# A two-layer graph network on one core: setup, middle and last stage rearranged, and the gathers' wait moved from a matmul to the transposes

## The chip, the cores and the metric

The kernel runs on one core of a Trainium2 chip. The time is that of the device in microseconds (us), the median of several runs. One further execution was taken with the hardware profiler, and all rows here are from that one. The engines are TensorE (PE, its weight loads PEld), VectorE (DVE), ScalarE (ACT), GpSimd (POOL) and SyncE (SP, which here only issues DMAs).

## The reference, cut to what matters

12,500 nodes with 16 features, and 412,500 edges sorted by their destination `dst`.

```python
h = relu(layernorm(x))
# layer 0: a weight matrix of each edge, from its 16 attributes
w = (relu(edge_attr_16 @ W1 + b1) @ W2 + b2).reshape(-1, 16, 16)
aggr = segment_sum(einsum('ei,eio->eo', h[src], w), dst)
out = aggr + h @ root + bias
x = x + relu((out - out.mean(0)) / sqrt(out.var(0) + 1e-5) * gamma + beta)
h = relu(layernorm(x))
# layer 1: messages from dst's features, summed by src
m = silu(einsum('ei,ej,ijh->eh', h[dst], edge_attr_8, W_msg_tp) * c1) @ W_msg_lin * c2
agg = segment_sum(m, src)
u = silu(einsum('ni,nh,ihk->nk', h, agg, W_upd_tp) * c3) @ W_upd_lin * c2
return x + h + u
```

## The kernel before

`build` (line 135) runs five stages with a barrier of all engines between them. Edges are worked on in G = 404 groups of 1,024, eight tiles of 128. Each engine's program is written out by hand in the order in which it runs, and engines wait for each other's semaphores (`wait_ge`, or `need`, which leaves out a wait for zero).

**Setup** (line 217). ScalarE issues the loads of `dst` and `src` in four chunks. VectorE makes the first layernorm (class `Norm`, line 543), whose square root ScalarE takes after it has rearranged W2 (line 438). `NodeLinear` (line 575) then multiplies all nodes in 13 chunks of 8 x 128 by b2 and `root`. Only then does VectorE turn `dst` into floats and find each group's least and greatest node (`front`, lines 342 to 348) and copy the turned `dst` out of PSUM (`dst_out`, line 350). GpSimd writes both index tables as int16 (`permute`), SyncE stores them, and the rows that layer 0 gathers (lines 278 to 281). `spread_in`, `spread_out` and a short chain give windows and the number of passes.

**Layer 0** (line 644). For each group GpSimd issues eight indirect DMAs, `xg <- gather_rows` (line 703), up to four groups ahead in a ring. TensorE's program for a group g (`body`, from line 834) is: `hidden` (line 801, W1, into ps_h), `edge_weights` (line 813, W2, into ps_w, four units of two tiles, a semaphore `wmm` after each unit), `hidden`, `edge_weights`, then `turn(g + 2)` (eight transposes of the attributes of a later group into ps_e, line 791, semaphore `e_turned`), and `scatter(g - 1)` (line 824, into ps_a). ScalarE evacuates ps_h with a relu (`relu`, line 742) and ps_e (`edges_T`, line 736). VectorE multiplies ps_w by the gathered rows and sums (lines 877 and 884). Two lines order the gathers:

```python
need(pool, q["msg_ready"], g - RING + 1)
need(pool, q["wmm"], 4 * (g - 2) + 3)
```

The second makes the gathers of group g wait for the third of the four units of group g - 2.

**Middle** (`between`, line 961). VectorE makes the batch norm, x + relu, and the second layernorm over [128, 104 x 16]. Then each node's 128 products Q = h @ Wmsg are made, and each is cut in three bf16 parts (high, middle, low), in 26 pieces of four node blocks: ScalarE writes high (line 1065), VectorE the residue (line 1039), ScalarE middle (line 1069), VectorE low (line 1044), SyncE stores Q (line 997).

**Layer 1** (line 1083). A block of its own copies and fills tables (`first_windows`, lines 1156 to 1168). In the loop SyncE loads four tiles for each group (`load`); after the loads of groups 1 and 2 it stores h and x by node (`by_node`, lines 1199 and 1201), and after group 3 reads them back in runs of nodes (`in_runs`). TensorE gathers Q rows by a one-hot product (line 1442), and sums messages by source in two ways (lines 1455 and 1468); GpSimd adds the first to tables in memory (line 1503).

**Last stage** (`finish`, line 1515). The tables are loaded and added (line 1588, half on VectorE, half on GpSimd), W_upd is loaded block-diagonally and rearranged by ScalarE (line 1682), and for 50 pairs of nodes per partition VectorE multiplies a PSUM bank by agg (line 1707) and reduces it (line 1714).

Of the kernel before, what the change touches and what calls it, by code (L numbers as in the profile page):

```python
# [26 lines left out]
P = 128  # L27
D = 16
# [41 lines left out]
def each_ring(engine, count, body, ring=4):  # L70


    for c in range(ring):
        body(c, c, 0)
    assert count % ring == 0
    with engine.Fori(0, (count - 2 * ring) // ring) as i:
        for u in range(ring):
            body(i * ring + (ring + u), u, i + 1)
    for u in range(ring):
        c = count - ring + u  # L80
        body(c, u, c // ring)
# [32 lines left out]
class Shapes:  # L114
    def __init__(self, n, e):
# [10 lines left out]
        self.BP = T * self.NC  # L126

# [10 lines left out]
def build(nc, x, src, dst, ea16, ea8, W1, b1, W2, b2, root, bias, gamma, beta,  # L138
          Wmsg, Wmsg_lin, Wupd, Wupd_lin, out):
    S = Shapes(x.shape[0], src.shape[0])  # L140
    with ExitStack() as ctx:
# [15 lines left out]
        k.q_rows = nc.dram_tensor("q_rows", (P * S.BP, 3 * P), bf16, kind="Internal").ap()  # L157
# [41 lines left out]
        with semaphores(nc) as sem:  # L199
            setup(nc, S, k, sem, src, dst, x, W1, b1, W2, b2, root, bias, gamma, beta)  # L200
        n_passes0 = nc.values_load(k.passes[0:1, 0:1], min_val=1, max_val=S.B // W + 1)
# [4 lines left out]
        with semaphores(nc) as sem, ExitStack() as c:  # L206
            k.Q = sb("Q", [P, S.BP, 3, P], bf16, c)
            between(nc, S, k, sem, c, Wmsg, Wmsg_lin, Wupd_lin)
        k.hp = sb("h_runs", [S.FP, S.FC, D], f32)
        k.xp = sb("x_runs", [S.FP, S.FC, D], f32)  # L210
        with semaphores(nc) as sem, ExitStack() as c:
            layer1(nc, S, k, sem, c, ea8, n_passes1)
        with semaphores(nc) as sem, ExitStack() as c:
            finish(nc, S, k, sem, c, Wupd, out)


def setup(nc, S, k, sem, src, dst, x, W1, b1, W2, b2, root, bias, gamma, beta):
# [3 lines left out]
    CH = len(chunks)  # L221
    with ExitStack() as c:
# [19 lines left out]
        pidx_i = sb("pidx_i", [P, 1], i32)  # L242
        rows = sb("rows", [P, S.BP, 2 * D], f32)
# [7 lines left out]
        reduced, masked = sem("reduced"), sem("masked")  # L251
# [5 lines left out]
        h_ready, rows_ready, stored = sem("h0_ready"), sem("rows_ready"), sem("rows_stored")  # L257
# [14 lines left out]
        def _(sp):  # L272
# [5 lines left out]
            sp.wait_ge(rows_ready, 1)  # L278
            sp.dma_start(k.rows[0:P * (S.B - 1), :].rearrange("(c p) f -> p c f", p=P),
                         rows[:, 0:S.B - 1, :]).then_inc(stored, 16)  # L280
# [8 lines left out]
            sp.wait_ge(stored, 32)  # L289
# [3 lines left out]
        def _(pool):  # L293
# [22 lines left out]
            for i, (g0, n) in enumerate(chunks):  # L316
                pool.wait_ge(s_flt, i + 1)
                permute(1, i, s_perm)
                if i == CH - 1:

                    pool.wait_ge(reduced, CH)
# [5 lines left out]
                else:  # L327
                    pool.wait_ge(d_flt, i + 1)
                permute(0, i, d_perm)

        @block.vector
        def _(v):
# [9 lines left out]
            def front(i):  # L342
                n = chunks[i][1]
                v.wait_ge(tab_in[0][i], landed(i))
                v.tensor_copy(flt[0][i][:, :], raw[0][i][:, :]).then_inc(d_flt, 1)
                v.wait_ge(d_flt, i + 1)
                v.tensor_reduce(lohi[0:n, i, 0:1], flt[0][i][:, :], X, ALU.min)
                v.tensor_reduce(lohi[0:n, i, 1:2], flt[0][i][:, :], X, ALU.max).then_inc(reduced, 1)

            def dst_out(i):  # L350
                g0, n = chunks[i]
                v.wait_ge(tr_d, i + 1)
                for h in range(2):
                    last = v.tensor_copy(k.dst[:, g0:g0 + n, 4 * h:4 * h + 4],
                                         ps_d[h][:, :, 0:n].rearrange("p t g -> p g t"))
                last.then_inc(ev_d, 1)
# [21 lines left out]
            v.wait_ge(nodes.packed, nodes.ALL)  # L378
# [9 lines left out]
            v.wait_ge(lin.taken, S.NC)  # L388
            v.sem_inc(rows_ready, 1)

            front(0)
            for i in range(1, CH):
                front(i)
                dst_out(i - 1)
# [11 lines left out]
            dst_out(CH - 1)  # L406
# [16 lines left out]
        def _(a):  # L423
# [10 lines left out]
            for i in range(CH):  # L434
                a.wait_ge(tab_in[1][i], landed(i))
                a.activation(flt[1][i][:, :], raw[1][i][:, :], ACT.Copy).then_inc(s_flt, 1)
# [3 lines left out]
            norm.scalar(a)  # L440
            lin.scalar(a)
            for i, (g0, n) in enumerate(chunks):
                a.wait_ge(tr_s, i + 1)
                for h in range(2):
                    last = a.activation(k.src[:, g0:g0 + n, 4 * h:4 * h + 4],
                                        ps_s[h][:, :, 0:n].rearrange("p t g -> p g t"), ACT.Copy)
                last.then_inc(ev_s, 1)

        @block.tensor
        def _(pe):  # L450
            pe.wait_ge(cst, 6)
            pe.wait_ge(nodes.packed, nodes.ALL)
            pe.wait_ge(h_ready, 1)
            lin.tensor(pe, k.ident[:, :])
            for i, (g0, n) in enumerate(chunks):
# [11 lines left out]
                last.then_inc(tr_d, 1)  # L467
            pe.wait_ge(ev_s, CH)
# [7 lines left out]
class NodesIn:  # L476


    def __init__(self, nc, S, k, sem, c):
        def sb(name, shape, dt):  # L480
# [4 lines left out]
        self.cleared, self.w_in, self.x_in, self.packed, self.dve, self.split = (  # L485
            sem(n) for n in ("cleared", "w_in", "x_in", "packed", "sn_dve", "w1split"))
        self.ALL = 16 * (2 * T + 6 + 6)
# [12 lines left out]
    def load_weights(self, sp, b1, W2, b2, root, bias, gamma, beta):  # L500
        k, packed = self.k, self.packed
# [1254 lines left out]
```

## Time and profile before

| | |
|---|---|
| median of 3 runs | 8827.98 us (8803.6 to 8840.02) |
| the profiled execution | 8860.82 us, span 8859.1 us |
| busy in it: PE, PEld | 7393.8 us (83%), 6326.6 us (71%) |
| DVE, POOL, ACT | 6501.9 us (73%), 5659.4 us (64%), 4441.1 us (50%) |
| mean granted clock of TensorE | 0.904 |

The span runs from the first to the last instruction. An engine's busy time is the union of its instructions; waits, branches and the issue of DMAs by SP and ACT are not in it. GpSimd's indirect DMAs are, for the time that it takes to make them. Shares over the whole span mix stages with different limits, so the stages are to be looked at one by one.

### The profile page before, as it was taken

How to read it: one execution, taken by the hardware profiler on the slowest of the kernel's cores; microseconds unless marked ns; L12 is line 12 of the kernel's file. 1: busy time of each engine (PE TensorE's matmuls, PEld its weight loads, DVE VectorE, ACT ScalarE, POOL GpSimd, SP SyncE). 2: the span in 40 equal slices, each digit the busy share in tenths (PEclk: the TensorE clock that was granted, in tenths of full speed). 3: DMA queues.
4: the chain of work that ended last, by engine and by line, in shares of the span. 5: the costliest groups of instructions: out<-in, count | busy, mean ns of one | idle time of the engine just before them, and what ended most of it. 6: DMA issues, size and time to landing. Idle time of an engine off the chain costs nothing. (4 is left out here: it accounts for less than half of the span.)

```text
span 8859.1 us, 189093 instructions
## 1 busy us (share of the span) xinstructions
PE 7393.8 (83%) x52097; PEld 6326.6 (71%) x52097; DVE 6501.9 (73%) x16875; ACT 4441.1 (50%) x8258; POOL 5659.4 (64%) x4883
## 2 busy tenths in 40 slices
PE   5777777777777777777777778599999999999997
PEld 4555665656665566665555656499999999999996
DVE  5555665656665566665565656799999999999997
ACT  2333333333333333333333333478888877778874
POOL 4555555555555555555555556288888888878884
PEclk8888888888888888888888888799999999999999
DMA  2000000000000000000000001444444455554443
GB/s 45 14 14 14 15 15 15 15 14 15 15 15 14 14 15 15 15 15 14 14 14 14 15 14 29 94 73 75 74 74 75 73 73 73 73 72 73 75 73 55
DMA packets 702285, 335.45 MB, mean 38 GB/s; under 512 B 422862, under 2 KB 645928, under 8 KB 702256
## 3 DMA queue, kind: packets, MB, share of 16 engines
q0 software_dynamic: 336128, 66.50, 12.4%
q1 hardware_dynamic: 364946, 265.19, 11.9%
q10 hardware_dynamic: 1182, 3.44, 0.1%
q8 instruction: 10, 0.16, 0.0%
q14 instruction: 19, 0.16, 0.0%
HBM read 301.49 MB, written 33.15 MB: 38 GB/s over the span
## 5 line engine op out<-in xcount | busy, mean ns | idle before, releaser
L703 POOL DMA_INDIRECT xg<-gather_rows,idx x3232 | 3082.3, 954 | 2385.2 <-PE ps_w L813 1140.4
L813 PE MATMUL ps_w<-W2s,hT 128*128 128x256 f32 x12928 | 3432.4, 417 | 446.2 <-issue 418.2
L813 PEld LDWEIGHTS ps_w<-W2s,hT 128*128 128x128 f32 x12928 | 2707.9, 210 | 1131.7 <-issue 687.0
L1503 POOL DMA_INDIRECT sums<-total,row x1616 | 2545.4, 1575 | 564.9 <-issue 440.8
L1468 PE MATMUL ps_wide<-hot_col,placed 128*128 128x392 f32 x12928 | 2439.0, 346 | 15.8 <-issue 9.6
L742 ACT ACTIVATE hT<-ps_h,b1c 128x512 f32<-128x512 f32 x1616 | 1018.6, 681 | 2721.4 <-remote 2163.2
L1468 PEld LDWEIGHTS ps_wide<-hot_col,placed 128*128 128x128 f32 x12928 | 2317.7, 196 | 29.8 <-issue 22.9
L877 DVE TENSOR_TENSOR prod<-ps_w,xg 128x512 f32<-128x512 f32 x1616 | 1095.9, 690 | 1118.0 <-remote 560.8
L1401 ACT ACTIVATE square<-iota_col,minus_col 128x784 bf16<-128x784 int16 x1212 | 1060.5, 937 | 88.5 <-issue 66.1
L1306 DVE SCALAR_TENSOR_TENSOR placed<-ps_r,src_r,halves 128x512 fp32r<-128x512 f32 x1616 | 1096.9, 740 | 0.1
L884 DVE TENSOR_REDUCE msg<-prod 128x32 f32<-128x512 f32 x1616 | 1059.1, 676 | 0.0
L801 PE MATMUL ps_h<-eT,W1p 96*128 96x512 bf16 x1616 | 562.9, 416 | 448.9 <-ACT eT L736 272.1
L1407 ACT ACTIVATE hot_col<-square,ones 128x2352 fp32r<-128x2352 bf16 x404 | 910.4, 2253 | 0.0
L908 DVE TENSOR_SCALAR hot<-iota,rel_t 128x256 bf16<-128x256 bf16 x3232 | 729.1, 298 | 113.2 <-DVE ea_res L860 58.7
L860 DVE TENSOR_TENSOR ea_res<-ea,ea_parts 128x128 f32<-128x128 f32 x404 | 116.7, 289 | 767.6 <-ACT ea_parts L723 542.2
L1442 PE MATMUL ps_q<-q_win,hotT 128*128 128x128 bf16 x9696 | 609.6, 220 | 28.0 <-DVE hotT L1245 28.0
L1263 DVE TENSOR_TENSOR prod<-ps_q,e 128x512 f32<-128x512 f32 x808 | 550.7, 682 | 80.6 <-issue 76.1
L801 PEld LDWEIGHTS ps_h<-eT,W1p 96*128 96x128 bf16 x1616 | 151.6, 99 | 626.9 <-issue 514.2
L1442 PEld LDWEIGHTS ps_q<-q_win,hotT 128*128 128x128 bf16 x9696 | 547.9, 98 | 29.1 <-issue 28.1
L1272 DVE TENSOR_REDUCE pre<-prod 128x64 f32<-128x512 f32 x808 | 546.8, 677 | 0.1
L824 PE MATMUL ps_a<-parts,hot 128*128 128x48 bf16 x6464 | 289.4, 184 | 300.7 <-issue 293.0
L824 PEld LDWEIGHTS ps_a<-parts,hot 128*128 128x128 bf16 x6464 | 230.1, 96 | 306.0 <-issue 298.8
(187 smaller groups left out, 4954.4 us busy)
## 6 DMA issues: line engine op xcount, KB each, us to landing
dst_row<-dst_rows SPq DMA_DIRECT2D x404, 256.0 KB
xg<-gather_rows,idx POOLq DMA_INDIRECT x3232
src_row<-src_rows SPq DMA_DIRECT2D x404, 128.0 KB
q_win<-q_rows SPq DMA_DIRECT2D x404, 96.0 KB
ea<-in_edge_attr SPq DMA_DIRECT2D x404, 64.0 KB
sums<-total,row POOLq DMA_INDIRECT x1616
e<-in_edge_attr SPq DMA_DIRECT2D x404, 32.0 KB
q_rows<-Q SPq DMA_DIRECT2D x13, 768.0 KB, 3.5
```

Of the source, the lines that this page charges most:

```text
L703: pool.indirect_dma_start(xg[r][:, t, :], None, k.rows, bass.IndirectOffsetOnAxis(ap=idx[r][:, t:t + 1], axis=0)).then_inc(xg_in[r][t], 16)
L742: a.activation(hT[s][:, j, :], ps_h[j][:, :], ACT.Relu, bias=k.b1[:, j:j + 1]).then_inc(q["relued"], 1)
L813: last = pe.matmul(bank[:, w, :, :].rearrange("p i o -> p (i o)"), hT[half][:, j, col:col + P], k.W2[:, j, :], start=(j == 0), stop=(j == 1))
L877: v.tensor_tensor(prod[u % 2][:, :, :, :], ps_w[u][:, :, :, :], xg[r][:, 2 * u:2 * u + 2, 0:D].unsqueeze(2).broadcast_to([P, 2, D, D]), AL ...
L884: v.tensor_reduce(msg[s][:, 2 * u:2 * u + 2, :], prod[u % 2][:, :, :, :], X, ALU.add).then_inc(q["reduced0"], 1)
L908: last = v.tensor_scalar(hot[s][:, t, :], k.iota[:, :], k.rel[:, bass.ds(g, 1), t:t + 1].rearrange("p g t -> p (g t)"), None, ALU.is_equal)
L1306: last = v.scalar_tensor_tensor(placed[s][:, w, :, :, :].rearrange("p r f a -> p r (f a)"), ps_r[:, :, :], src_r[:, bass.ds(g, 1), w], hal ...
L1401: last = a.activation(square[:, n, :], iota_col[:, :], ACT.Square, bias=minus_col[:, bass.ds(g, 1), WIDE - ACT_TILES + n])
L1407: a.activation(hot_col[s][:, WIDE - ACT_TILES:, :, :].rearrange("p w a b -> p (w a b)"), square[:, :, :].rearrange("p w b -> p (w b)"), AC ...
L1442: last = pe.matmul(ps_q[u][:, w, :, :].rearrange("p h j -> p (h j)"), hotT[s][:, t * P:(t + 1) * P], q_win[s][:, part * P:(part + 1) * P], ...
L1468: last = pe.matmul(ps_wide[:, 2 * r + a, 0:S.LC], placed[s][:, w, r * HR:(r + 1) * HR, :, part].rearrange("p r f -> p (r f)"), hot_col[s][ ...
L1503: pool.indirect_dma_start(k.sums[t], bass.IndirectOffsetOnAxis(ap=row[r][:, t:t + 1], axis=0), total[r][:, t, :], None, compute_op=ALU.add ...
```

## The change

- **Layer 0:** the gathers of group g wait for `e_turned` of g, the transposes at the end of TensorE's program for g - 2. The tables of sources that layer 1 opens with are made by VectorE in layer 0's last four groups.
- **Setup:** the least and greatest are found from the integers before the layernorm; ScalarE converts both tables and empties both sets of banks; TensorE turns them before `NodeLinear`; the relu is folded in the scaling; W2 is rearranged last; GpSimd copies h into the rows; these are stored in two halves.
- **Middle:** 98 node blocks and not 104; squares by ScalarE in halves; mask only on the last block; relu and the addition to x as one; Q in 25 pieces, every third high part by VectorE, all middle parts by ScalarE, all low parts by GpSimd; x is stored by node here; x + h is left to the last stage.
- **Layer 1:** no table block; the first `dst_row` load goes ahead of the wait for the windows; h is stored and read after the last group's loads; W_upd is loaded and rearranged by ScalarE before its first group; ScalarE's first two laps of four are written out.
- **Last stage:** tables in three pieces, loads issued by SyncE and ScalarE; from the fourth chunk on GpSimd folds each product to half its width before VectorE reduces it; four product buffers instead of two, reduce two behind.

```diff
@@ setup, VectorE @@
-            front(0)
-            for i in range(1, CH):
-                front(i)
-                dst_out(i - 1)
...
+            for i in range(CH):
+                least_greatest(i)
             v.wait_ge(nodes.x_in, 32)
             norm.vector(v, link, k.x, k.h)
             v.sem_inc(h_ready, 1)
-            v.tensor_copy(rows[:, :, 0:D], k.h[:, :, :])
@@ setup, ScalarE @@
+            for i in range(CH + 1):
+                if i < CH:
+                    to_float(1, i, s_flt)
+                    to_float(0, i, d_flt)
+                if i >= 1:
+                    out_of_psum(i - 1, k.src, ps_s, tr_s, ev_s)
+                    out_of_psum(i - 1, k.dst, ps_d, tr_d, ev_d)
+            norm.scalar(a)
+            lin.scalar(a)
@@ layer 0, GpSimd, gather(g) @@
                     need(pool, q["msg_ready"], g - RING + 1)
-                    need(pool, q["wmm"], 4 * (g - 2) + 3)
+                    pool.wait_ge(q["e_turned"], g + 1)
@@ layer 0, VectorE, end of body(g) @@
+                    if isinstance(g, int) and g >= G - RING:
+                        source_tables(g - (G - RING))
@@ middle, GpSimd @@
+        for piece in range(NP4):
+            b0 = 4 * piece
+            pool.wait_ge(n["q_mid"], piece + 1)
+            pool.tensor_tensor(k.Q[:, b0:b0 + 4, 2, :], res[piece % 3][:, :, :], k.Q[:, b0:b0 + 4, 1, :],
+                               ALU.subtract).then_inc(n["q_lo"], 1)
@@ middle, VectorE @@
+            if piece % 3 == 2:
+                v.wait_ge(lin.done, piece + 1)
+                v.tensor_copy(k.Q[:, b0:b0 + 4, 0, :], y).then_inc(n["q_hi_v"], 1)
@@ layer 1, SyncE @@
-                    if isinstance(g, int) and g == 1:
-                        by_node(k.h_rows, k.h)
-                    if isinstance(g, int) and g == 2:
-                        by_node(k.x_rows, k.x)
...
                 each(sp, G, body, head=4, tail=2)
+                store_by_node(sp, S, k.h_rows, k.h, q["h_stored"])
+                sp.wait_ge(q["h_stored"], 32)
+                in_runs(k.hp, k.h_rows)
@@ layer 1, ScalarE, before its first group @@
+                a.wait_ge(q["bdu_clear"], 1)
+                for b in range(T):
+                    a.dma_start(bd_hk[D * b:D * (b + 1), b, :],
+                                Wupd.rearrange("i h k -> i (h k)")).then_inc(q["bdu_in"], 16)
+                a.wait_ge(q["bdu_in"], 16 * T)
@@ last stage @@
-    SPLIT = ((0, MID), (MID, FC))
+    SPLIT = ((0, 2 * T), (2 * T, 6 * T), (6 * T, FC))
+    RU = 4
+    WHOLE = 3
...
+        for n in range(FOLD0, len(pairs)):
+            pool.wait_ge(upd_taken, n + 1)
+            need(pool, reduced, n - RU + 1)
+            y = prod[n % RU]
+            pool.tensor_tensor(fold[n % RU][:, :, :, :], y[:, :, :, 0:D // 2], y[:, :, :, D // 2:],
+                               ALU.add).then_inc(folded, 1)
```

On GpSimd, at the gathers of layer 0, the order stood thus before (`wmm` counts units of edge weights, `msg_ready` the messages done):

```order
L703 DMA xg<-gather_rows,idx 128x32 [waits idx_ready,wmm]
L703 DMA xg<-gather_rows,idx 128x32 x7
L76 UNCONDITIONAL_BRANCH
L76 ISA
L54 REGISTER_ALU [waits idx_ready]
L54 ISA [waits msg_ready]
L703 DMA xg<-gather_rows,idx 128x32 [waits wmm]
```

and now:

```order
L716 DMA xg<-gather_rows,idx 128x32 [waits idx_ready,e_turned]
L716 DMA xg<-gather_rows,idx 128x32 x7
L76 UNCONDITIONAL_BRANCH
L76 ISA
L54 REGISTER_ALU [waits idx_ready]
L716 DMA xg<-gather_rows,idx 128x32 [waits msg_ready,e_turned]
```

Nothing else in the loop moved: the same eight DMAs, another semaphore ahead of the first.

On ScalarE, at the first pieces of Q in the middle (`msg_xT` the turned nodes, `msg_po` the products in PSUM, `q_res` the residue), before:

```order
L620 ACTIVATE msg_xT<-msg_pt 128x128 [waits msg_turned] x2
L1065 ACTIVATE Q<-msg_po 128x4x128 [waits msg_done] x2
L1069 ACTIVATE Q<-q_res 128x4x128 [waits msg_taken] x2
L620 ACTIVATE msg_xT<-msg_pt 128x128 [waits msg_done,msg_turned]
L1065 ACTIVATE Q<-msg_po 128x4x128 [waits msg_done] x2
```

and now:

```order
L632 ACTIVATE msg_xT<-msg_pt 128x128 [waits msg_turned] x2
L1155 ACTIVATE Q<-msg_po 128x4x128 [waits msg_done] x2
L1145 ACTIVATE Q<-q_res 128x4x128 [waits msg_taken]
L632 ACTIVATE msg_xT<-msg_pt 128x128 [waits msg_done,msg_turned]
L1145 ACTIVATE Q<-q_res 128x4x128 [waits msg_taken]
L1155 ACTIVATE Q<-msg_po 128x4x128 [waits msg_done]
```

The middle part of a piece (L1145) now follows the high part of the next piece, and every third high part is gone from this engine.

On SyncE, after the second group's loads of layer 1, before (`h_rows` is h stored by node):

```order
L1191 DMA dst_row<-dst_rows 128x1024
L1194 DMA src_row<-src_rows 128x512
L1199 DMA h_rows<-hn 128x97x16
L1201 DMA h_rows<-hn 84x16
L1185 TENSOR_LOAD win_i [waits same_ready,gathered,hotT_ready,mult1]
```

and now:

```order
L1261 DMA e_1<-in_edge_attr 128x64
L1243 DMA dst_row<-dst_rows 128x1024
L1266 DMA src_row<-src_rows 128x512
L1258 TENSOR_LOAD win_i [waits same_ready,gathered,hotT_ready,mult1]
L1258 ISA x2
```

The two stores stand no more between the loads of groups 1 and 2 (nor those of x between 2 and 3).

## Rows read from the trace of the kernel before

**Rows 1.** By stage: length, busy us of each engine (instructions), TensorE clock, DMA share, GB/s.

```profile
84.00:5557.00 5473.00, 4212.03 (x24240) 3286.35 (x24240) 3345.43 (x9297) 1924.10 (x4040) 3082.34 (x3232) 0.86 0.09 15
5558.70:5594.00 35.30, 1.22 (x4) 1.00 (x4) 32.60 (x23) 2.48 (x3) 1.21 (x3) 0.50 0.02 2
5594.00:5641.30 47.30, 29.46 (x65) 11.49 (x65) 35.39 (x53) 31.06 (x65) 0.00 (x0) 0.90 0.64 216
5641.30:5651.40 10.10, 0.00 (x0) 0.00 (x0) 8.50 (x10) 0.00 (x0) 0.79 (x1) 0.50 0.00 1
...
5693.50:8752.10 3058.60, 3038.97 (x27320) 2958.61 (x27320) 2938.39 (x7227) 2431.40 (x4018) 2541.01 (x1615) 1.00 0.50 73
...
8763.70:8859.00 95.30, 63.11 (x191) 31.48 (x191) 70.00 (x117) 19.26 (x66) 9.58 (x5) 0.86 0.18 52
```

**Rows 2.** The page's group of layer 0's gathers: busy, mean ns, idle ahead of them.

```profile
L703 POOL DMA_INDIRECT xg<-gather_rows,idx x3232 | 3082.3, 954 | 2385.2 <-PE ps_w L813 1140.4
```

**Rows 3.** What ended the idle time ahead of those gathers: us in total, times.

```profile
  PE ps_w L813: 1140.4, 199
...
  remote: 335.4, 155
```

**Rows 4.** Timeline of GpSimd, start, us, idle before: first (once last) gather of groups.

```profile
1881.99 0.94 POOL L703 DMA_INDIRECT xg<-gather_rows,idx  x1 [2.41 <-remote]
...
1894.15 0.94 POOL L703 DMA_INDIRECT xg<-gather_rows,idx  x1 [2.41 <-remote]
...
1904.84 0.94 POOL L703 DMA_INDIRECT xg<-gather_rows,idx  x1 [0.47 <-issue]
...
1913.59 0.94 POOL L703 DMA_INDIRECT xg<-gather_rows,idx  x1 [0.30 <-issue]
1922.83 0.94 POOL L703 DMA_INDIRECT xg<-gather_rows,idx  x1 [8.29 <-PE ps_w L813]
```

**Rows 5.** Timeline of TensorE in the same stretch.

```profile
1901.64 0.61 PE L791 MATMUL ps_e<-identb,ea_parts 128*96 128x128 bf16 x8
...
1911.22 0.58 PE L813 MATMUL ps_w<-W2s,hT 128*128 128x256 f32 x1 [0.62 <-issue]
...
1916.15 3.73 PE L813 MATMUL ps_w<-W2s,hT 128*128 128x256 f32 x8 [0.81 <-issue]
```

**Rows 6.** Timeline of ScalarE in the same stretch.

```profile
1894.28 1.27 ACT L742 ACTIVATE hT<-ps_h,b1c 128x512 f32<-128x512 f32 x2 [5.30 <-PE ps_h L801]
...
1917.10 1.26 ACT L742 ACTIVATE hT<-ps_h,b1c 128x512 f32<-128x512 f32 x2 [16.55 <-remote]
```

**Rows 7.** Timeline of VectorE in the setup.

```profile
35.63 0.80 DVE L565 RECIPROCAL ln_sd<-ln_sd 128x104 f32<-128x104 f32 x1 [8.06 <-ACT ln_sd L571]
...
52.64 0.69 DVE L345 CAST fltd<-rawd 128x1024 f32<-128x1024 int32 x1 [0.15 <-DVE aggn L384]
...
70.77 0.15 DVE L397 CAST lohi_i<-lohi 128x8 int32<-128x8 f32 x1
```

**Rows 8.** Timeline of ScalarE and VectorE at Q's last pieces.

```profile
5630.77 1.29 DVE L1039 TENSOR_TENSOR q_res<-msg_po,Q 128x512 f32<-128x512 f32 x2
...
5631.59 1.23 ACT L1069 ACTIVATE Q<-q_res 128x512 f32 x2 [0.60 <-DVE q_res L1039]
```

**Rows 9.** Timeline of SyncE's queue at the start of layer 1: issue and its length.

```profile
5659.47 10.22 SPq L1201 DMA_DIRECT2D h_rows<-hn  x1
```

**Rows 10.** Timeline of the last stage.

```profile
8768.52 0.96 DVE L1588 TENSOR_TENSOR acc<-acc,table 125x768 f32<-125x768 f32 x1 [14.57 <-DMA table<-sums]
...
8775.45 3.66 ACT L1682 ACTIVATE bd_upd<-bd_hk 128x2048 f32<-128x2048 f32 x1 [18.60 <-DMA bd_hk<-in_L_gnn_W_upd_tp]
8775.99 8.21 POOL L1588 TENSOR_TENSOR acc<-acc,table 125x832 f32<-125x832 f32 x4 [10.48 <-DMA table<-sums]
...
8782.29 0.69 DVE L1707 TENSOR_TENSOR uprod<-ps_upd,agg_lin 125x512 f32<-125x512 f32 x1 [8.65 <-PE ps_upd L1625]
...
8786.02 0.68 DVE L1714 TENSOR_REDUCE u<-uprod 125x32 f32<-125x512 f32 x1
```

More of the change, by code:

```diff
@@ L221, in setup @@
     CH = len(chunks)
+    HALF = S.NC // 2
     with ExitStack() as c:
@@ L340, in _, with least_greatest @@
             nodes.vector(v)
-            def front(i):
+            def least_greatest(i):
                 n = chunks[i][1]
                 v.wait_ge(tab_in[0][i], landed(i))
[L345 to L356, printed above, removed]
+                v.tensor_reduce(lohi[0:n, i, 0:1], raw[0][i][:, :], X, ALU.min)
+                v.tensor_reduce(lohi[0:n, i, 1:2], raw[0][i][:, :], X, ALU.max).then_inc(reduced, 1)
             def spread_in(i):
@@ L603, in product @@
             for j in range(self.pieces):
+                if self.last is not None and c * self.pieces + j >= self.last:
+                    continue
                 need(pe, self.taken, c * self.pieces + j + 1 - self.ring)
@@ L1070, in _, with mid @@
-        lin.copy(a, 0, 0)
-        each(a, S.NC, parts, head=3 - S.NC % 2, tail=1)
+        for i, (b0, b1) in enumerate(HALVES):
+            a.wait_ge(n["ln_centred"], i + 1)
+            if i == 0:
+                a.wait_ge(n["bn_part"], 3)
+            a.activation(sq[:, b0:b1, :], k.h[:, b0:b1, :], ACT.Square).then_inc(n["ln_squared"], 1)
+        a.wait_ge(n["ln_var"], 1)
+        a.activation(lsd[:, :], lvar[:, :], ACT.Sqrt).then_inc(n["ln_sd"], 1)
+        def mid(piece):
+            a.wait_ge(lin.taken, piece + 1)
+            a.activation(k.Q[:, 4 * piece:4 * piece + 4, 1, :], res[piece % 3][:, :, :], ACT.Copy
+                         ).then_inc(n["q_mid"], 1)
@@ new lines, in _ @@
+        lin.copy(a, 0, 0)
+        for piece in range(NP4):
+            ch, j, b0 = piece // 2, piece % 2, 4 * piece
+            if j == 0 and ch + 1 < S.NC:
+                lin.copy(a, ch + 1, (ch + 1) % 2)
+            if piece % 3 != 2:
+                a.wait_ge(lin.done, piece + 1)
+                a.activation(k.Q[:, b0:b0 + 4, 0, :],
+                             lin.bank(ch % 2, j)[:, :].rearrange("p (b w) -> p b w", w=P),
+                             ACT.Copy).then_inc(n["q_hi_a"], 1)
+            if piece >= 1:
+                mid(piece - 1)
@@ L1073, in _ @@
+        mid(NP4 - 1)
     @block.tensor
     def _(pe):
[L1075 to L1077 removed]
+        pe.wait_ge(n["bn_part"], 1)
+        pe.matmul(ps_m[:, 0, :], k.ones[:, :], sums[:, 0, :], start=True, stop=True).then_inc(n["bn_sum"], 1)
+        pe.wait_ge(n["bn_part"], 3)
+        for i in range(2):
+            last = pe.matmul(ps_m[:, 1, :], k.ones[:, :], sums[:, 1 + i, :], start=(i == 0), stop=(i == 1))
@@ L1720, in result @@
                                    ).then_inc(out_ready, 1)
-        pairs = [(ch, j) for ch in range(NF) for j in range(nodes(ch) // 2)]
         for i, (ch, j) in enumerate(pairs):
-            if j == 0 and ch >= 2:
+            if j == 1 and ch >= 2:
                 result(ch - 2)
             product(ch, j)
-            if i >= 1:
-                reduce(*pairs[i - 1])
+            if i >= 2:
+                reduce(*pairs[i - 2])
+        reduce(*pairs[-2])
         reduce(*pairs[-1])
```

407 lines of the change are left out of this document (222 added, 185 removed).

## The prediction

> **What bounds the kernel now.** I read the stages first, as busy time by stretch [rows 1]. Layer 0 takes 5473 us for 404 groups, 13.5 us each, and nobody is full: TensorE 77%, VectorE 61%, GpSimd 56%, and TensorE's clock is 0.86 on the mean. Layer 1 takes 3059 us with TensorE busy in 99% of it at full clock: what frees other engines there is worth nothing. The rest is the setup (84 us), the middle and the table block (5557 to 5693) and the last stage (95 us), where VectorE does most of the work.
>
> So layer 0 is where time can be found, and the reader should ask what closes its loop. GpSimd makes eight gathers in a row, each 0.94 us with 0.30 us between, 9.7 us in all [rows 4]. They are 3232 with 2385.2 us of idle time ahead of them [rows 2]; seven of eight follow after 0.30 us, 2828 x 0.30 = 848 us, so the 404 first gathers wait 2385 - 848 = 1537 us, **3.80 us each**. What ended it was `ps_w` of TensorE 199 times, 5.7 us on the mean, and 155 times a semaphore with no record of its giver, 2.2 us on the mean [rows 3]. These are two different states. In the timeline most groups start about 2.4 us after the last; but the group of 1904.84 starts after only 0.47 us, and then the one after it waits 8.29 us and starts 18.0 us later [rows 4].
>
> The rows of TensorE show why [rows 5, 6]. By its records the transposes were issued at 1901.64, but while the early gathers run TensorE comes forward by about one matmul per gather: single matmuls of `ps_w` with 0.6 us of idle time between them, and no run of them before 1916.15, after the last gather of 1913.59. ScalarE's relu waits 16.55 us, to 1917.10. By contrast, in the groups that start after 2.41 us the relu comes 0.13 us after the first gather (1894.28 and 1894.15) and the loop takes 12.2 us. I read: gathers hold TensorE's progress, and the release comes 1.5 to 2 us after the last gather of a group. If GpSimd starts the next eight before TensorE has drained what it was held with, the hold lasts for a further 10 us. The old condition (third unit of four) lets that happen, since one unit and the transposes are still to come.
>
> A rule speaks against this. The Trainium skill (SBUF — State Buffer, section on its two separate sides) says that TensorE, ScalarE and VectorE's own port pair never wait on anyone and that DMA and engine ports cannot contend; by it the gathers could not slow TensorE, the layer 0 term below would be zero, and the sum would be the first rival's 8795 us. The single matmuls above differ from it, whatever path the hold takes.
>
> **The change part by part.**
>
> *Gathers.* The new wait adds the fourth unit and eight transposes to the condition. That is 1.9 us at full clock (8 matmuls take 3.73 us at half of it, [rows 5]) and 0.61 us for the transposes [rows 5], 2.5 in all. In the usual state it costs near nothing, as the four units and the transposes were already done under the gathers and come free together. In the short starts it moves the gathers 2 to 3 us and takes away the 8 to 10 us wait of the next. I take 2.6 us ahead of every group: the 2.41 seen twice [rows 4] and 0.2 for the later semaphore. (3.80 - 2.60) x 404 = **-485 us**. Ends: 2.2 us, the mean of the 155 [rows 3], gives -646; if the 199 whose wait TensorE ended pay the whole 2.5 us on top of 2.2, the mean is 3.43 and the gain 149.
> *Layer 0's ends.* The first gathers wait for the first transposes, which come within half a loop (6.8 us), once; VectorE takes over the table block's 8.5 us [rows 1] in four groups, where it is busy 61% of the time, so most is hidden. **+8** (0 to 15).
> *Setup.* From 52.64 to 70.77 VectorE does `front` and `dst_out` [rows 7]: 18.1 us, gone to ScalarE and to the time in which VectorE still waits for x. The reciprocal waits 8.06 us because ScalarE rearranges W2 first [rows 7]: 7.7 of it goes, and 1 us of relu. **-27** (-15 to -30). Cover: ScalarE's conversions and GpSimd's copies of 2 us each must be through by the time of the chain; SyncE's 10 us of storing rows is begun earlier by halves. If the stores are late, they are the next to end the stage.
> *Norms.* 35.3 us of a VectorE chain [rows 1] loses two masks, two squares and two relus (9.6 us at 1.9 or 1.0 each) and 6% of its width, and gains four short waits: **-10** (-6 to -13).
> *Q.* Today the 26 pieces and the barrier take 47.3 us [rows 1]: of each, VectorE makes a residue of 0.65 (two in 1.29) and a low part like it, ScalarE a middle part of 0.62 (two in 1.23) and a high part like it, with waits of 0.6 us for each other [rows 8]. Now a piece costs VectorE 0.65 x 4/3 = 0.87, ScalarE 0.62 + 0.62 x 2/3 and half a copy, 1.15, and GpSimd one subtraction of 512, which from 8.21 / 4 for 832 [rows 10] is 1.26 plus a wait, 1.37. GpSimd bounds: 25 x 1.37 and the same 9 us of head, tail and barrier, 43: **-4** (-9 if ScalarE bounds, +8 at 1.85 us).
> *Table block.* 10.1 us [rows 1], now nothing between the barriers: **-10** (-8 to -11).
> *Start of layer 1.* A store holds SyncE 10.22 us [rows 9], and there are two, each ahead of a group's loads; a steady group takes 3058.6 / 404 = 7.57 us [rows 1], and as loads are two ahead I count 15 of the 20 us as lost. But ScalarE must first get W_upd, which in the last stage took 11.75 us from the stage's start to the copy (8763.70 to 8775.45) and 3.66 for it [rows 1, 10]; of these 15.4 us some 9 lie beside the first loads and products, so 6 are left. **-9** (-15 to 0). Behind this ScalarE queue stand group 0's squares and columns, for which TensorE waits. The store of h moves to the end of the loop, under its last two groups.
> *Layer 1's loop:* 404 groups at 7.57, TensorE bound, **0**.
> *Last stage.* First product at 8782.29; the tables' four adds begin at 8768.52, and ScalarE's 3.66 us copy at 8775.45 is what is waited for [rows 10]. With it gone and a smaller first piece the product starts at about 8773: -9. A pair costs VectorE 0.69 + 0.68 us [rows 10]; a half-wide reduce would save some 0.3 of it for 38 pairs, 11 us. But over 12.5 chunks TensorE is busy 63.11 / 12.5 = 5.05 us each and VectorE 70.00 / 12.5 = 5.6 [rows 1], so TensorE bounds soon and 9.5 chunks x 0.55 = 5 us come. **-14** (-6 to -20).
>
> Sum: -485 + 8 - 27 - 10 - 4 - 10 - 9 - 14 = -551. Against the profiled execution's own 8861: 8310 us. That execution is 33 us above the median of the three runs; part of such a spread must be in the number of long waits, which go, so I say **8300 us**. A measurement of this kernel can tell about 0.5% (44 us) from no change.
>
> **The rivals.**
> *The hold does not come from the early start, or is only moved:* long waits stay as often, layer 0 as before, the rest -66: **8795**. For it: the skill's rule, and that I know no path by which GpSimd stops TensorE. Against: 18 us loops follow 0.47 us starts [rows 4]. 9%.
> *Slower:* the gathers are 9.7 us in a row and close the loop, so a later start is paid in full where it buys nothing. If TensorE is held for a fixed time after each start and the new condition adds the unit and the transposes to each wait, it is 404 x 2.5 = +1010, less 66: **9805**. It decides when the mean wait ahead of a group's first gather passes 3.80 + 66 / 404 = 3.96 us. For it: the 199 waits that TensorE ended [rows 3]. Against: in the 2.41 us state the relu's wait ends with the gather's start, so all was through by then [rows 4, 6]. 5%.
> *The small stages give nothing* (GpSimd beside VectorE, SyncE's stores and ScalarE's W_upd eat their gains): 8861 - 485 + 0 = **8376**. 9%.
>
> **How the numbers follow.** Forecast 77%; the rivals 9, 5 and 9%. The forecast's own range goes from 8861 - 646 - 66 = 8149 to 8861 - 149 - 66 = 8646, since the wait's two ends dominate; it holds 8376 too. I give 8160 to 8640 and leave out 8795 and 9805, with some of the tails. Faster by over 0.5%: 92% (half of the first rival counts: 8795 is 0.4 to 0.7% lower). Within 0.5%: 3%. Slower: 5%.
>
> **What would show it.** Gathers' idle time near 404 x 2.6 + 848 = 1900 us and no wait of 8 to 10 us ahead of one; ScalarE's `hT` waits of 16 us gone; layer 0 near 4990 us; its TensorE clock above 0.86. Layer 0 starting 27 us earlier; no tables between the middle and layer 1; GpSimd in Q at 1.3 us; the first product 10 us after the last stage's start (18.6 now, [rows 1, 10]). Wrong if the mean wait ahead of the first gather stays at 3.8 us, or if relu waits grow.

## The result, and the profile after

The changed kernel took **8396.4 us** (median of four runs, 8381.9 to 8402.8), the kernel before 8834.0 us beside it (8803.6 to 8880.5): ratio **0.948**, 95% interval 0.944 to 0.953. The forecast was 8300 us, between 8160 and 8640. The profiled execution took 8394.6 us; its span is 8392.9 us, against 8859.1 before: 466.2 us less.

First the stages, as in [rows 1]: layer 0, the norms, Q, the end of Q's stage, the start of layer 1, layer 1's loop, the last stage. Columns: length, busy us of TensorE, its weight loads, VectorE, ScalarE and GpSimd, TensorE's clock, DMA share, GB/s.

```profile
70.70:5121.70 5051.00, 4117.76 (x24232) 3322.56 (x24232) 3341.49 (x9296) 1931.90 (x4035) 3151.26 (x3232) 0.91 0.09 16
5123.80:5153.90 30.10, 3.20 (x9) 2.23 (x10) 23.82 (x25) 6.14 (x9) 3.37 (x5) 0.50 0.45 30
5153.90:5183.80 29.90, 26.45 (x61) 10.40 (x59) 22.12 (x33) 24.70 (x53) 25.55 (x23) 0.93 0.77 238
5183.80:5193.90 10.10, 0.00 (x0) 0.00 (x0) 0.00 (x0) 0.58 (x1) 2.46 (x3) 0.56 0.88 271
5193.90:5217.00 23.10, 8.53 (x84) 7.76 (x84) 15.22 (x35) 14.92 (x17) 1.80 (x1) 0.50 0.35 92
5217.00:8301.30 3084.30, 3064.95 (x27401) 2971.38 (x27401) 2936.91 (x7246) 2437.94 (x4038) 2570.54 (x1616) 1.00 0.48 73
8301.30:8392.90 91.60, 63.24 (x193) 31.51 (x192) 57.11 (x118) 16.15 (x69) 40.37 (x46) 0.89 0.22 62
```

Two of these rows are cut at other places than in [rows 1]. Layer 1's loop, from its first product into `ps_wide` to its last, took 3076.0 us before and 3084.3 now; from that last product to the end of the program it was 102.8 us and is 91.6.

The gathers' group, which answers to [rows 2], and from the list of that line its durations and what ended its idle time, which answers to [rows 3]:

```profile
L716 POOL DMA_INDIRECT xg<-gather_rows,idx x3232 | 3151.3, 975 | 1917.6 <-issue 1865.2
```

```profile
L716 POOL DMA_INDIRECT xg<-gather_rows,idx x3232: 949/955/1477, 70.7 to 5104.8; - x191
  issue: 1865.2, 3226
  PE ps_e L804: 42.5, 2
```

The idle time fell from 2385.2 to 1917.6 us, which is what was forecast (1900). But the busy time rose from 3082.3 to 3151.3: the gathers themselves got longer. Over the 403 steps from one group's first gather to the next, the step went from 13.51 to 12.47 us; in it the wait from 3.71 to 2.51 us and the row of eight gathers from 9.79 to 9.96 us. The two states are gone with it: before, 60 of the 403 waits were under 1 us, and 59 of these were followed by one of over 8 us (84 such in all); now 399 of 403 lie between 1 and 3.4 us, and one is over 8.

The timeline of GpSimd, first and last gathers of groups (compare [rows 4]):

```profile
1905.75 0.95 POOL L716 DMA_INDIRECT xg<-gather_rows,idx  x1 [0.30 <-issue]
1909.29 0.95 POOL L716 DMA_INDIRECT xg<-gather_rows,idx  x1 [2.58 <-issue]
...
1918.10 0.95 POOL L716 DMA_INDIRECT xg<-gather_rows,idx  x1 [0.30 <-issue]
1921.75 0.95 POOL L716 DMA_INDIRECT xg<-gather_rows,idx  x1 [2.70 <-issue]
```

Nearly every group is now of one kind: about 2.6 us of wait, where before 0.47 us was followed by 8.29 us. ("Issue" says only that the view found no giver. The trace's semaphore records do: 401 of 402 first gathers start less than 1.2 us, most of them 0.76 us, after a record of `e_turned`.) TensorE in the same stretch ([rows 5] before):

```profile
1914.10 3.62 PE L826 MATMUL ps_w<-W2s,hT 128*128 128x256 f32 x16
1917.55 0.61 PE L804 MATMUL ps_e<-identb,ea_parts 128*96 128x128 bf16 x8
1918.00 0.41 PE L837 MATMUL ps_a<-parts,hot 128*128 128x48 bf16 x10
1919.32 0.18 PE L837 MATMUL ps_a<-parts,hot 128*128 128x48 bf16 x1 [0.91 <-issue]
1920.74 0.29 PE L837 MATMUL ps_a<-parts,hot 128*128 128x48 bf16 x5 [1.23 <-issue]
```

And VectorE, which takes the products up:

```profile
1915.01 1.29 DVE L890 TENSOR_TENSOR prod<-ps_w,xg 128x512 f32<-128x512 f32 x2
1916.21 0.68 DVE L897 TENSOR_REDUCE msg<-prod 128x32 f32<-128x512 f32 x1
1920.82 0.69 DVE L890 TENSOR_TENSOR prod<-ps_w,xg 128x512 f32<-128x512 f32 x1 [3.94 <-remote]
```

Two things are to be seen. The hold is still there, once in every group: the two units recorded from 1914.10 on are through by 1917.7, but VectorE gets the first of them only at 1920.82, 1.8 us after the last gather ended (1918.10 + 0.95). The record of `e_turned`, too, comes 1.8 us after the last gather's end on the median, in 399 of 403 groups between 1.0 and 2.5 us, though the transposes are recorded before (here they are through at 1918.16, and their report comes at 1920.98). That closes the loop: the gathers wait for a report which comes only when they have ended. And the records say more than I had read in them: the semaphore records of the product units come at 1920.80 and 1920.89, two units in 0.09 us, where TensorE needs 1.73 us for one. So by its records TensorE had done the work by then; what was late was its report. It goes on until ten of the sixteen small scatter matmuls are out, and only then pauses, 0.91 and 1.23 us, with a single matmul between.

### The profile page after: what moved, and what is told of

Same layout as the page of the kernel before. It is cut to its first block and busy times, and to the rows that moved or that the text cites. A ratio compares the mean times of both kernels' runs of the same rounds, so it can differ in the third digit from the quotient of the medians.

```text
span 8392.9 us, 188590 instructions
## 1 busy us (share of the span) xinstructions
PE 7312.4 (87%) x52097; PEld 6366.3 (76%) x52097; DVE 6441.9 (77%) x16842; ACT 4455.1 (53%) x8265; POOL 5818.6 (69%) x4952
## 3 DMA queue, kind: packets, MB, share of 16 engines
q0 software_dynamic: 336128, 66.50, 11.8%
## 5 line engine op out<-in xcount | busy, mean ns | idle before, releaser
L716 POOL DMA_INDIRECT xg<-gather_rows,idx x3232 | 3151.3, 975 | 1917.6 <-issue 1865.2
L826 PE MATMUL ps_w<-W2s,hT 128*128 128x256 f32 x12928 | 3352.5, 416 | 143.9 <-issue 131.9
L837 PE MATMUL ps_a<-parts,hot 128*128 128x48 bf16 x6464 | 351.5, 183 | 582.6 <-issue 569.4
L837 PEld LDWEIGHTS ps_a<-parts,hot 128*128 128x128 bf16 x6464 | 255.5, 96 | 606.2 <-issue 593.1
L814 PE MATMUL ps_h<-eT,W1p 96*128 96x512 bf16 x1616 | 519.3, 394 | 206.1 <-issue 165.3
L765 ACT ACTIVATE parts<-msg_res 128x128 bf16<-128x128 f32 x404 | 125.5, 311 | 558.0 <-DVE msg_res L909 309.7
L749 ACT ACTIVATE eT<-ps_e 96x1024 bf16<-96x1024 bf16 x404 | 409.3, 1013 | 1.9 <-PE ps_e L804 1.9
```

The costliest lines, as they stand in the source:

```text
L716: pool.indirect_dma_start(xg[r][:, t, :], None, k.rows, bass.IndirectOffsetOnAxis(ap=idx[r][:, t:t + 1], axis=0)).then_inc(xg_in[r][t], 16)
L826: last = pe.matmul(bank[:, w, :, :].rearrange("p i o -> p (i o)"), hT[half][:, j, col:col + P], k.W2[:, j, :], start=(j == 0), stop=(j == 1))
```

## The experiments

The twelve kernels ran in four sets, each on a chip of its own, with the kernel before beside them. That turned out to matter: the kernel before took 8842, 7429, 8840 and 7421 us in the four sets. I call the first and third chip *holding*, the others *free*. The result above came from runs with 8834 us for the kernel before, so from a holding one.

**Which part of the change did it?** `e1_wait_only`, the kernel before with one line:

```
-                    need(pool, q["wmm"], 4 * (g - 2) + 3)
+                    pool.wait_ge(q["e_turned"], g + 1)
```

> The kernel before with the one new wait (gathers wait for the group's transposes). Theory (the wait alone ends the 18 us loops): a group goes from 13.5 to 12.5 us as in the changed kernel, idle time ahead of a group's first gather 3.7 to 2.5 us, layer 0 shorter by some 420 us, time near 8834 - 420 = 8414 us. Rival (the other edits share in it, by what they shift): less than half of that, above 8600 us.

Measured: 8396.3 us, ratio 0.952 (0.948 to 0.955). `e2_rest_only`, the changed kernel with that line put back:

> The changed kernel with the old wait (third unit of four). Theory: layer 0 as before, 13.5 us a group with as many waits of 8 to 11 us; setup, middle, start of layer 1 and last stage as in the changed kernel, so 8834 less 40 to 66: 8770 to 8795 us. Rival (the other edits change layer 0's rhythm): below 8700 us.

Measured: 8847.8 us against 8842.0, ratio 1.003 (1.000 to 1.005). The wait alone gives the whole gain, to within a microsecond of the changed kernel's own measurement, and the rest of the change gives nothing that the times show. Yet the rest's stages did get shorter: in e2's trace the first product of layer 0 starts 24.3 us earlier than before, from layer 0's last addition to layer 1's first product into `ps_wide` it is 95.5 us instead of 123.8, and after layer 1's last product 92.1 instead of 102.8. That is 63 us. In the traces layer 0 took more than half of it back: from its first to its last product it is 34 us longer than before, and e2's execution ends 21 us earlier. The medians do not show even that (6 us the other way), but the kernel before alone spread over 8785 to 8863 us. The gathers' group of the page, first of e1, then of e2:

```profile
L703 POOL DMA_INDIRECT xg<-gather_rows,idx x3232 | 3108.8, 962 | 1887.1 <-issue 1846.2
```

```profile
L716 POOL DMA_INDIRECT xg<-gather_rows,idx x3232 | 3119.1, 965 | 2395.3 <-PE ps_w L826 1184.1
```

With the rest, the gathers' busy time rises in both settings: from 3082.3 to 3119.1 us under the old wait, from 3108.8 to 3151.3 under the new one. The medians show that a part of it is in every one of them; e1's list of the line (min, median, max in ns), against 949/955 above:

```profile
L703 POOL DMA_INDIRECT xg<-gather_rows,idx x3232: 938/944/1282, 96.2 to 5069.7; - x191
```

The median is 944 ns in both kernels without the rest and 952 or 955 ns in all that have it and still gather; e2, on e1's chip, has 952. Eight ns by 3232 gathers are 26 us, eleven are 36. The size is not firm: the changed kernel itself, run again as e9, has 952 ns and 3116.9 us busy instead of 3151.3. Why the gathers get longer (buffers lie elsewhere, in SBUF and in DRAM) was not tried.

**Is it the gathers that hold TensorE?** `e3_half_gathers` leaves out every second gather (the rows that are not gathered are filled once with a constant, and VectorE no longer waits for them, here and in e5 and e6; not shown):

```
-                    for t in range(T):
+                    for t in range(0, T, 2):
                         pool.indirect_dma_start(
```

> The changed kernel with four of a group's eight gathers left out (the other half of the gathered rows is a constant). Theory (TensorE is held until the gathers have ended, and the gathers wait for it: 9.96 + 2.5 us is the loop): the loop is no longer the gathers' and falls to what TensorE itself needs, some 10 us (32 products at 0.22, the hidden layer, transposes and scatters), so about 404 x 2.2 = 900 us less than 8396: near 7500 us. Rival (the chain TensorE, ScalarE, VectorE sets 12.46 us and the gathers only fit into it): 8396 as before, with a wait of 7 us ahead of a group's first gather.

Measured: 7091.8 us. GpSimd and TensorE:

```profile
1503.01 0.95 POOL L716 DMA_INDIRECT xg<-gather_rows,idx  x1 [4.39 <-issue]
...
1512.11 0.95 POOL L716 DMA_INDIRECT xg<-gather_rows,idx  x1 [4.39 <-issue]
```

```profile
1506.99 3.62 PE L829 MATMUL ps_w<-W2s,hT 128*128 128x256 f32 x16
1510.69 0.65 PE L807 MATMUL ps_e<-identb,ea_parts 128*96 128x128 bf16 x8
1511.17 0.56 PE L840 MATMUL ps_a<-parts,hot 128*128 128x48 bf16 x16
1511.58 0.60 PE L817 MATMUL ps_h<-eT,W1p 96*128 96x512 bf16 x2
```

A group takes 9.24 us and nothing of TensorE is held any more: its sixteen scatter matmuls go in 0.56 us. The time fell by 1305 us, 3.2 us a group, more than the 2.2 expected, since TensorE needs less than I thought. Part of that is the clock. In the changed kernel TensorE pauses under the gathers, and after the pause its granted clock is the lower of its two levels (1.2 and 2.4 GHz): 0.50 of full speed from 1908.70 to 1911.70, so that the sixteen products recorded from 1908.72 take 5.10 us and those from 1914.10 take 3.62. It was at that level for 878 us of layer 0 (1525 us in the kernel before), in e3 for 13. So the chain of semaphores alone does not make 12.46 us; with eight gathers it does, and four in a row do no harm.

`e4_no_dma` puts an addition of about the same length in each gather's place:

```
-                        pool.indirect_dma_start(
-                            xg[r][:, t, :], None, k.rows,
-                            bass.IndirectOffsetOnAxis(ap=idx[r][:, t:t + 1], axis=0)
-                        ).then_inc(xg_in[r][t], 16)
+                        pool.tensor_tensor(pad[t][:, :], pad[8][:, :], pad[9][:, :],
+                                           ALU.add).then_inc(xg_in[r][t], 1)
```

> The changed kernel with each gather replaced by an addition on GpSimd of about the same length (384 columns, estimated 0.95 us from 2.05 us for 832), with no DMA; the gathered rows are a constant. Theory (it is the gather's transfer or its making of descriptors that holds TensorE): TensorE is not held, a group takes what TensorE needs, 10 to 10.5 us, near 7550 us. Rival (any work of GpSimd holds it, by a port or a lock it shares): 12.4 us a group, 8400 us. Second rival: VectorE's operations get longer beside GpSimd's and nothing else, 8000 us.

Measured: 7698.2 us, 10.74 us a group. GpSimd is as busy as with gathers, and TensorE is not held. VectorE closes this loop. Its groups from 1000 to 3000 us (busy us, mean ns, idle before), first of this kernel, then of e1:

```profile
L879 DVE TENSOR_TENSOR ea_res<-ea,ea_parts 128x128 f32<-128x128 f32 x186 | 201.4, 1083 | 0.0
L909 DVE TENSOR_TENSOR msg<-msg,xg 128x128 f32<-128x128 f32 x186 | 118.2, 635 | 6.4
```

```profile
L860 DVE TENSOR_TENSOR ea_res<-ea,ea_parts 128x128 f32<-128x128 f32 x162 | 47.2, 292 | 75.5 <-issue 49.8 <-ACT ea_parts L723 25.6
```

A subtraction of 0.29 us takes 1.08 beside GpSimd's additions of 1.01. All VectorE's groups together come to 1935 us for 186 groups, 10.4 of the 10.74 us. This looks like a wait for a port, and it strikes VectorE alone: the products and reductions that read PSUM keep their 689 and 676 ns. The Trainium skill (SBUF — State Buffer, section on its two separate sides) says just this: one exclusive lock, between VectorE and GpSimd, and TensorE waits on nobody; here the trace agrees. So what delays TensorE under gathers is not an SBUF port that GpSimd's computing would take too.

**Where does the hold begin, and is it the transfers?** Four kernels were made for this: `e5_four_late` (four gathers, held back until the second product unit of the next group), `e6_six_gathers`, `e7_split` (all eight, the last four held back by the same condition) and `e8_plain_dma` (SyncE's plain transfers for gathers).

Their edits, in this order (e7's follows below, with e10's):

```
+                    need(pool, q["wmm"], 4 * (g - 1) + 2)
...
-                    for t in range(T):
+                    for t in (0, 2, 4, 6):
```

```
-                    for t in range(T):
+                    for t in (0, 1, 2, 3, 4, 5):
```

```
+                    for t in range(T):
+                        sp.dma_start(xg[r][:, t, :],
+                                     k.rows[t * P:(t + 1) * P, :]).then_inc(xg_in[r][t], 16)
...
-                    for t in range(T):
-                        pool.indirect_dma_start(
-                            xg[r][:, t, :], None, k.rows,
-                            bass.IndirectOffsetOnAxis(ap=idx[r][:, t:t + 1], axis=0)
-                        ).then_inc(xg_in[r][t], 16)
```

> The changed kernel with four of a group's eight gathers left out, and the four that are left held back until the second of the next group's four product units. Theory C (TensorE is held only once more than four gathers follow each other): 9.2 us a group as with four early gathers, near 7090 us. Theory P (it is the second half of TensorE's group that is held, whichever gathers run then): third and fourth unit, transposes and scatters come 1.8 us after the last gather, so some 4.4 + 5 + 1.8 = 11 us a group, near 7800 us.

> The changed kernel with two of a group's eight gathers left out. Under C and P alike, if the hold lasts until 1.8 us after the last gather: 6 x 1.25 + 2.5 = 10 us a group, near 7400 us. If there is no hold with six either: 9.24 us a group, 7090 us.

> The changed kernel with all eight gathers, the last four held back until the second product unit of the next group. If each four start a new count (C): no hold, GpSimd's own 9.96 us and two short starts bound the group, about 10.9 us, near 7770 us. If the hold depends on the gathers of the last 10 us or on the place: 12.5 us or up to 13 us a group, 8400 to 8600 us.

> The changed kernel with each gather replaced by a plain transfer of 128 rows in order, of the same size and landing in the same place, issued by SyncE with the same waits; GpSimd only counts. What is computed is another sum. If the hold comes from GpSimd's making of the gathers' descriptors: no hold, 9.2 to 9.5 us a group, 7100 to 7200 us. If it comes from the transfers of 128 short rows: 12 us a group or more, above 8200 us.

Measured: 7057.2, 7079.0, 7386.6 and 7048.9 us, with the kernel before at 7429.3. The chip was a free one, and there the four tell nothing of the hold, as there is none. What they tell is the free chip's own limit: three run at TensorE's 9.24 to 9.31 us a group, and the one with all gathers at GpSimd's. Its page:

```profile
L719 POOL DMA_INDIRECT xg<-gather_rows,idx x3232 | 3082.0, 954 | 1018.6 <-issue 983.4
```

983.4 / 3232 is the 0.30 us by which nearly every gather follows its forerunner; 8 x 1.26 = 10.06 us a group, without a pause. The kernel before, which is 7429 us there, should have run so too: less its other stages (97.7 + 102.8 + 123.8 us) and layer 1's loop, 3044 us in these four, some 4060 us are left, 10.05 a group. No trace of it on a free chip was kept, so this is a sum and not a reading. **By it the new wait gains nothing on a free chip**; neither e1 nor the changed kernel was run on one.

So the changed kernel and e7 ran once more. The edit of e7 and e10:

```
                     for t in range(T):
+                        if t == T // 2:
+                            need(pool, q["wmm"], 4 * (g - 1) + 2)
+                            pool.sem_inc(q["gathers_begun"], 1)
                         pool.indirect_dma_start(
```

> The changed kernel once more, since in the last four runs the kernel before itself took 7429 us where it had taken 8842: on that chip nothing seems to hold TensorE. If this lands on a chip of that kind: GpSimd's own 8 x 1.26 = 10.06 us a group bound both kernels, the wait buys nothing, and only the stages' 63 us remain: 7429 - 55 = 7375 us, ratio 0.992. If on one of the first kind: 8396 us, ratio 0.95.

> The changed kernel with the last four gathers of a group held back until the second product unit of the next. On a chip that does not hold TensorE: 7386 us as before. On one that does: C (four gathers in a row do no harm, a new count begins after the wait) 10.1 to 10.9 us a group, 7450 to 7770 us; if the hold goes by the gathers of the last 10 us or by the place in TensorE's group, 12.5 to 13 us a group, 8400 to 8600 us.

This chip was a holding one, and not the first. e9: 8317.5 us against 8840.0, ratio 0.942 (0.937 to 0.947), so the gain stands on a second chip. e10: 8402.3 us, ratio 0.951 (0.945 to 0.956), 85 us slower than e9 and 12.51 us a group: the split buys nothing. GpSimd and TensorE of e10:

```profile
1509.60 1.04 POOL L719 DMA_INDIRECT xg<-gather_rows,idx  x1 [0.30 <-issue]
1510.94 0.95 POOL L719 DMA_INDIRECT xg<-gather_rows,idx  x1 [0.30 <-issue]
...
1514.71 0.95 POOL L719 DMA_INDIRECT xg<-gather_rows,idx  x1 [0.30 <-issue]
1517.97 0.95 POOL L719 DMA_INDIRECT xg<-gather_rows,idx  x1 [2.31 <-issue]
```

```profile
1513.27 0.54 PE L840 MATMUL ps_a<-parts,hot 128*128 128x48 bf16 x15
1514.19 0.18 PE L840 MATMUL ps_a<-parts,hot 128*128 128x48 bf16 x1 [0.38 <-issue]
1515.62 0.38 PE L817 MATMUL ps_h<-eT,W1p 96*128 96x512 bf16 x1 [1.25 <-issue]
```

It was no fair test of the count: the second unit was mostly through when the fifth gather came (0.30 us of pause at 1510.94, 0.63 on the mean of all groups), so eight gathers still stood in a row. The last set repeated the plain transfers and the four late gathers for a holding chip.

> The plain transfers once more, for a chip on which the kernel before takes 8840 us. If the hold comes from GpSimd's making of the gathers' descriptors: no hold, 9.24 us a group, 7050 to 7100 us, and no two reports of product units within 0.3 us of each other. If it comes from the transfers of 128 short rows: 12 us a group or more, above 8200 us. (Where the kernel before takes 7430 us, this says nothing.)

> Four gathers held back until the second product unit once more, for a chip on which the kernel before takes 8840 us. Theory C (the hold begins some 5 us, or four gathers, into a row of gathers): 9.24 us a group, near 7090 us. Theory P (what is held is the second half of TensorE's group, whichever gathers run then): 11 us a group, near 7800 us.

Measured: 7045.0 and 7052.1 us, with the kernel before at 7420.6: a free chip again. Both questions stay open: whether the hold begins after some gathers in a row or in the second half of TensorE's group, and whether plain transfers would cause it. No version that leaves nothing out beat the changed kernel on a holding chip, and on a free one the changed kernel itself was not run.

## Why the prediction was right, point by point

*What bounds layer 0.* Right in what it does, not in what it is. GpSimd's early starts made the long waits, and the one new condition ended them (e1). I wrote that "gathers hold TensorE's progress"; on the two holding chips they delay first its reports, then its issue. That the release comes 1.5 to 2 us after the last gather is borne out: 1.8 us on the median. On a free chip they do neither (e7, with all eight gathers), and that there are such chips the one profile could not have told me.

*Gathers, -485.* The wait was to fall from 3.80 to 2.60 us; counted over the steps it fell from 3.71 to 2.51, 1.21 x 403 = 487 us. (The 3.80 took every pause in a row as 0.30 us; the first of each row is 0.335.) What I had left out is that the gathers' own length is not a constant: +0.17 us for each row of eight, +69 us on the page. It has two parts. e1 shows 26.5 us (3108.8 against 3082.3): in the even rhythm the third to fifth gather often stand beside VectorE's one-hot tiles, and those are the long ones: 348 of e1's gathers took over 1 us, 342 of them at these three places, and 152 in the kernel before. The other 42.5 us are the changed kernel's against e1's; in e9, the same kernel, they are 8, so how much of them the rest of the change costs is open between 8 and 43 us. *Layer 0's ends, +8:* its length from first product to last addition fell by 411 us, and 403 steps of 1.04 us are 419: the ends cost the 8.

*Setup, -27:* first product of layer 0 at 74.1 instead of 97.7, -24. The 8.06 us wait of [rows 7] is gone; VectorE's timeline now:

```profile
32.41 0.80 DVE L575 RECIPROCAL ln_sd<-ln_sd 128x104 f32<-128x104 f32 x1 [0.35 <-ACT ln_sd L580]
```

*Norms, -10:* 30.1 instead of 35.3 us, -5: the chain got shorter, but the waits for ScalarE's squares and for the two small products ate half. *Q, -4, and table block, -10:* from the norms' end to the barrier's end 40.0 us instead of 57.4, -17. Q came out better than its term because GpSimd's subtraction was cheaper than I scaled it. Its timeline, against the forecast's 1.26 us and a wait of 0.11:

```profile
5160.51 25.75 POOL L1030 TENSOR_TENSOR Q<-q_res,Q 128x512 bf16<-128x512 f32 x23 [0.21 <-ACT Q L1145]
```

That is 1.12 us a piece, with no idle time between: GpSimd bounds Q as forecast. *Start of layer 1, -9:* 28.9 to 23.1 us, -6. *Layer 1's loop, 0:* +8, as in e1, which has none of the edits there (3083.3 us; e2 3080.8, e9 3075.8): no effect of the change.

*Last stage, -14:* -11. The first product comes 8.8 us after the stage's first load (8308.62), 10 were forecast, 18.6 before:

```profile
8317.41 0.69 DVE L1797 TENSOR_TENSOR uprod<-ps_upd,agg_lin 125x512 f32<-125x512 f32 x1 [3.90 <-PE ps_upd L1717]
```

From there to the end it is 75.5 us instead of 76.8, so the 5 us of the chunks came to 1.3: TensorE, 63.24 us busy against 63.11, bounded them all.

*The sum:* -24 - 411 - 28 + 8 - 11 = -466, forecast -551. Of the 85 us between them 69 are the gathers' length.

*The rivals.* "The hold is only moved" is out on the holding chips: of the changed kernel's 403 waits two were over 3.4 us, of the kernel before's 97. The skill's rule behind it is not refuted, though: it is one of ports, e4 agrees with it, and the hold lies elsewhere. "Slower" needed a mean wait above 3.96 us; it is 2.51. "The small stages give nothing" was wrong in each stage and right in the sum: they gave 63 us, and e2 is not faster than the kernel before, since layer 0 took more than half of it back. This rival's 8376 us is nearer to the measured time than the forecast's 8300.

*What would show it:* the gathers' idle time, TensorE's clock in layer 0 (0.91, above 0.86) and the start of the last stage came as written. Layer 0 took 5051 us and not 4990, as the gathers got longer. ScalarE's waits for `hT` of 16 us are gone but for one of 13.6.

*Range and chances:* 8396 lies almost in the middle of the range (8400), but that middle is no forecast of mine: the range held the rival of 8376 too, and its width, not the sum, took in the 96 us by which the sum was off. The chances do not add up either: with half of the first rival, "faster by over 0.5%" is 77 + 9 + 4.5 = 90.5% and "within" 4.5%, not 92 and 3. And it was luck that both the profile I read and the result came from chips that hold TensorE: that a second kind exists, for which I would expect quite another answer, stood in no chance of mine.

## What to carry to other kernels

Where an engine starts its next round before those it disturbs have drained, one later wait can be worth more than all the arithmetic moved between engines, as on the holding chips here: find it by sorting the rounds by what the wait ahead of them was, not by their mean. A change can alter the price of an instruction that it doesn't touch; compare its median duration before and after, not only the stages edited. And run the kernel before beside each experiment: only its 7429 and 7421 us showed that six of mine could say nothing of the hold.

## What the hardware did that I had not expected

*Chips differ by 19% on this kernel.* The kernel before took 8834 to 8842 us on the holding chips and 7421 to 7429 on the free ones; layer 1's loop took 3076 to 3084 and 3040 to 3047 us. Whether it is the chip, its host or how the execution is recorded that differs, no run here tells.

*Reports come late, and some are missing.* Between 100 and 3800 us of the changed kernel the trace has 1186 product units with 919 semaphore records, of which 163 come within 0.3 us of the one before, though the units are 1.73 us apart at least (before: 1097, 943, 287; e1: 1200, 940, 130). In e7 there are 1472 of 1472 and no such pair. On the holding chip records are missing in e3 too (1283 of 1599), which is not held, and none in e4, which has no gathers (1378 of 1379). And they are missing for every engine: in the changed kernel's layer 0 the trace has 3655 of VectorE's 6849 records of this kind and 2475 of ScalarE's 4027, and of the 51,712 that the gathers' transfers give some 12,000; e7 on a free chip lacks one of VectorE's and none of the others. In layer 1, where no engine is held, ScalarE has 2399 of 3222 on the holding chip and 3190 on the free one. So what is short on those chips is at least the recording of semaphores, and missing records alone do not mean a hold.

*The transfers are no slower there.* The DMA packets tell it, of which both traces have the same 336,128 on the gathers' queue: the last packet of a gather ends 2.05 to 2.12 us after the gather's start on the median, at each of the eight places of a row, in the changed kernel, and 2.05 to 2.09 us in e7. So it is no queue of transfers that fills up.

*Whether an execution that is not recorded would be held too is open.* All times here come with a span and a clock of each execution, so all were recorded in some way. The Trainium skill (NOTIFIC — the notification-queue block, section on overflow) says that the block which writes such records pushes back on the engines that produce them rather than lose one inside. By that rule TensorE, whose matmuls and weight loads are recorded one by one, could be slowed by the recording itself. In its favour, every trace from a holding chip lacks many records, and those from free chips few or none. Missing records do not fit the rule that none is lost inside, unless these are lost behind the block. No run here decides it.

*GpSimd's gathers wait too.* The long ones, up to 1.25 us and more, stand beside VectorE's one-hot tiles: of the gathers that overlapped an operation of `hot` in the changed kernel 353 of 878 took over 1 us, of those that overlapped a reduction of the products into `msg` none of 1374. It is so on free chips too: in e5, where the third gather falls there in nearly every group, 385 of its 404 are over 1 us.
